# The second expert product in rounded parts, from the 13th tile on

## The chip, the cores and the metric

One core of a Trainium2 chip runs the whole program. The metric is device time in microseconds (us) of that core; lower is better. Engines: PE is TensorE (PEld its weight loads), ACT is ScalarE, DVE is VectorE, POOL is GpSimd, SP issues DMAs.

## What is computed

The input x holds 8 sequences of 512 tokens, 256 wide. First comes x + attention(layernorm(x)), a gated linear attention. The change does not touch it. Then comes a mixture of 8 experts with one expert per token:

```python
aff = x @ centroids.T
assign = jnp.argmax(aff, axis=1)
...
for e in range(nE):
    h = _layernorm(xs, ln_g[e], ln_b[e])
    h = jax.nn.relu(h @ w1[e].T + b1[e])      # 256 -> 1024
    ye = xs + h @ w2[e].T + b2[e]             # 1024 -> 256
    y = y + jnp.where((es == e)[:, None], ye, 0.0)
out_sorted = alpha * y + (1.0 - alpha) * xs
```

Everything is float32. The change is in h @ w2[e].T.

## The kernel before

The attention takes one sequence per step, with up to three sequences in flight. Each finished token is stored as a row of 514 words (normed x, base value, gate, token number) in rows_by_expert, sorted by expert. The second stage, which starts inside the last attention step, takes 39 tiles of 128 rows, all rows of a tile having the same expert. Every engine walks the tiles through its own function turn(t), written out by hand: tiles 0 to 11 one by one among the last attention work, then 20 tiles in a loop of 4 per round, then the last 7 written out. Each instruction waits on semaphores (need), and each engine works strictly in the order in which its turn lists things. In turn(t):

- PE (turn, L1180): up(t+1), 16 products of w1 with the tile's normed rows into bank_a (L1160); z_transposes(t+2), two transposes of gathered rows into bank_b (L1148); down(t), 8 products of 256 columns of h_act with w2_sb into one of two banks bank_l (L1176).
- ACT (turn, L882): relu(t), two ACTIVATEs of 512 columns (L880), then gains(t+2), two of 128 columns that read the transposes (L870).
- DVE (turn, L1565): the first half of bias_h(t+1) (L1548, it reads bank_a into h_sb), finish(t-1) (L1557 adds b2 out of bank_l, L1562 scales and adds the base value), the second half of bias_h(t+1).
- POOL (turn, L673): scatter(n), which waits for finish(n) and stores the tile to out (L667, L670); then gather(n+4), which waits for the same finish and fetches the rows of tile n+4 (L661) into the buffer that finish(n) has read. Four buffers go round.
- SP (fetch_w1, L503): after up(n) is done, 1 MB of w1 for tile n+4 goes into the same of four buffers (L509). w2 of all experts stays in SBUF.

bank_a is single: up(t+1) may write its first half only when bias_h(t) has read it, and so for the second half. h_sb and h_act are single too.

Of the kernel before, what the change touches and what calls it, by code (L numbers as in the profile page):

```python
# [54 lines left out]
def before(s, n):  # L55

    v = s.par - n
    return Step(s.half + v // s.of, v % s.of, s.of)


def number(s):
    return s.half * s.of + s.par


def need(eng, sem, per, s, k):

    base = per * s.par + k + 1
    if not isinstance(s.half, int):  # L70
        eng.wait_ge(sem, s.half * (s.of * per) + base)
    elif s.of * per * s.half + base > 1:
        eng.wait_ge(sem, s.of * per * s.half + base)
# [7 lines left out]
def build_program(nc, x, wq, wk, wv, wo, wg1, wg2, norm_w, centroids_t, ln_g, ln_b, w1_t, b1, w2_t, b2, out):  # L81
# [30 lines left out]
    with ctx:  # L112
        def sb(name, shape, dt):
            return ctx.enter_context(nc.sbuf_tensor(name, shape, dt))

        def sem(name):
            return ctx.enter_context(nc.semaphore(name))
# [2 lines left out]
        w2_sb = sb("w2_sb", [P, E * FC * D], F32)  # L120
        PHASE1_AB = 24576
        ARENA = 33808
        arena_at = nc.sbuf_base
        arena = sb("arena", [P, ARENA], F32)

        class Layout:

# [54 lines left out]
        gathered = [lay3.take(RW + 2)[:, 0:RW] for _ in range(SLOTS)]  # L182
        h_sb = lay3.take(F)
        h_act = lay3.take(F)

        earlier = lay2.take(P)
        is_max = lay2.take(TJ * E)
# [15 lines left out]
        per_tile = lay2.take(7 * TS)  # L205

        k_mix = [sb(f"k_mix{i}", [P, PAIRS * P], F32)[:, :] for i in range(2)]
        b2_sb = lay3.take(E * D)
        ident = sb("ident", [P, P], F32)
        ones = sb("ones", [P, P], F32)  # L210
        masks = sb("masks", [P, LEVELS * NCH * HALF], U8)
# [118 lines left out]
        s_h = sem("h_done")  # L330
        s_hb = sem("h_biased")
        s_hr = sem("h_ready")
        s_ye = sem("y_done")
        s_yb = sem("y_biased")
        s_yo = sem("y_ready")
# [94 lines left out]
        def expert_of(t):  # L430
            if isinstance(t.half, int):
                return tile_expert[0:1, number(t):number(t) + 1]
            return tile_expert[0:1, bass.ds(number(t), 1)]
# [19 lines left out]
        def rounds(eng, turn):  # L453


            with eng.Fori(NA // SLOTS, LAST - 1) as r:
                for i in range(SLOTS):
                    turn(Step(r, i, SLOTS))
            for i in range((LAST - 1) * SLOTS, TILES):
                turn(Step(i // SLOTS, i % SLOTS, SLOTS))  # L460

        def exists(t):

            return not isinstance(t.half, int) or number(t) < TILES
# [233 lines left out]
        def _(act):  # L698
# [163 lines left out]
            def gains(t):  # L862

                if isinstance(t.half, int):
                    act.wait_ge(s_idx, 1 if number(t) < NA else 3)
                e = act.value_load(expert_of(t), min_val=0, max_val=E - 1)
                need(act, s_zt, 1, t, 1)
                need(act, s_h, 2, before(t, 2), 2)
                for i in range(DC):
                    act.activation(xl_t[t.par % 2][:, i * P:(i + 1) * P], bank_b[0][:, i * P:(i + 1) * P], ACT.Identity,  # L870
                                   bias=b_col[:, bass.ds(e * DC + i, 1)], scale=g_col[:, bass.ds(e * DC + i, 1)]).then_inc(s_xl, 1)

            def relu(t):


                need(act, s_ye, 1, t, 0)
                for i in range(2):
                    need(act, s_hb, 2, t, i + 1)
                    w = slice(i * F // 2, (i + 1) * F // 2)
                    act.activation(h_act[:, w], h_sb[:, w], ACT.Relu).then_inc(s_hr, 1)  # L880

            def turn(t):  # L882
                relu(t)
                if exists(before(t, -2)):
                    gains(before(t, -2))

            x_norm(Step(0, 0, 2))
            pipeline(act, step)

            act.wait_ge(s_small, 64)  # L890
            need(act, s_pick, 2 * LEVELS, LAST_SEQ, 2 * LEVELS)
            gains(tile(0))
            gains(tile(1))
# [19 lines left out]
        def _(pe):  # L913
# [251 lines left out]
            def down(t):  # L1165

                p = t.par % 2
                if isinstance(t.half, int):
                    pe.wait_ge(s_idx, 1 if number(t) < NA else 3)
                e = pe.value_load(expert_of(t), min_val=0, max_val=E - 1)  # L1170

                need(pe, s_yb, 1, before(t, 2), 1)
                for k in range(FC):
                    if k % 4 == 0:
                        need(pe, s_hr, 2, t, k // 4 + 1)
                    m = pe.matmul(bank_l[p][:, 0:D], h_act[:, k * P:(k + 1) * P], w2_sb[:, bass.ds(e * (FC * D) + k * D, D)],  # L1176
                                  start=(k == 0), stop=(k == FC - 1))
                m.then_inc(s_ye, 1)

            def turn(t):  # L1180
                if exists(before(t, -1)):
                    up(before(t, -1))
                if exists(before(t, -2)):
                    z_transposes(before(t, -2))
                down(t)

            pe.wait_ge(s_const, 1)
            pe.wait_ge(s_wqk, 32)
# [31 lines left out]
        def _(dve):  # L1220
# [167 lines left out]
            def slots(c):  # L1388

                n = number(c)  # L1390
                need(dve, s_rank, 1, c, 1)
                if n in (EARLY - 1, NSEQ - 1):
                    dve.wait_ge(s_total, 1 + (n == NSEQ - 1))
                    own(dve.tensor_copy(end_e, bank_c[1][:, E * TJ:E * (TJ + 1)]))
                dve.tensor_tensor(by_e(place), bank_c[1][:, 0:E * TJ].rearrange("p (e j) -> p j e", e=E),
                                  hot5[:, :, 1:TJ + 1].rearrange("p e j -> p j e"), ALU.mult).then_inc(s_slot, 1)
                need(dve, s_slot, 2, c, 1)
                dve.tensor_reduce(slot_f[:, n * TJ:(n + 1) * TJ], by_e(place), AX_X, ALU.add).then_inc(s_slot, 1)
# [153 lines left out]
            def finish(t):  # L1552
                p = t.par
                e = dve.value_load(expert_of(t), min_val=0, max_val=E - 1)
                need(dve, s_ye, 1, t, 1)
                need(dve, s_yo, 1, t, 0)
                dve.tensor_tensor(y_sb, bank_l[p % 2][:, 0:D], b2_sb[:, bass.ds(e * D, D)], ALU.add).then_inc(s_yb, 1)  # L1557
                need(dve, s_yb, 1, t, 1)

                if not isinstance(t.half, int) or t.half > 0:  # L1560
                    dve.wait_ge(s_out[p], t.half * 16)
                dve.scalar_tensor_tensor(out=y_out[p], in0=y_sb, scalar=gathered[p][:, 2 * D:2 * D + 1],  # L1562
                                         in1=gathered[p][:, D:2 * D], op0=ALU.mult, op1=ALU.add).then_inc(s_yo, 1)

            def turn(t):  # L1565
                one = before(t, -1) if exists(before(t, -1)) else None
                if one is not None:
                    bias_h(one, 0)
                if not isinstance(t.half, int) or number(t) > 0:
                    finish(before(t, 1))  # L1570
                if one is not None:
                    bias_h(one, 1)

            c = LAST_SEQ
            slots(LAST_BUT_ONE)
            for n in range(2):
                bias_h(tile(0), n)
# [58 lines left out]
```

## Time and profile before

| | us |
|---|---|
| median of 3 runs | 653.22 (652.31 to 654.06) |
| the profiled execution | 650.17 |
| its span | 648.4 |
| PE busy | 593.3 (92%) |
| DVE, ACT, POOL busy | 346.1, 281.5, 260.8 |
| granted TensorE clock, mean share of full speed | 0.975 |

The span runs from the first to the last instruction of the profiled execution; 1.8 us of that execution's time lie around it. The page gives busy time of each engine and groups of instructions by line; the trace can also be asked for a timeline, for windows (busy time, granted clock and DMA share of a stretch) and for single lines. "Idle before <- releaser" on a row tells how long the engine stood still before it and what ended that; "issue" is idle time that no wait explains, such as the reading of a register.

### The profile page before, as it was taken

The page shows a single profiled execution, that of the slowest core. Times are in us where ns is not written, and L with a number is a line of the kernel's source. Part 1 is how long each engine was busy: PE and PEld are TensorE (multiplying, and loading weights), DVE is VectorE, ACT ScalarE, POOL GpSimd, SP SyncE. Part 2 cuts the span into 40 slices and gives each one's busy share as a digit, 9 for nine tenths or more (in the row PEclk, how much of TensorE's full clock was granted, in tenths as well). Part 3 has the DMA queues.
Part 4 walks back from the last instruction along what each step waited for, and adds up shares of the span by engine and source line. Part 5 has one row for each costly group of instructions (what it writes and reads, how often), then busy time and mean ns, then how long its engine had stood idle before and what let it go on. Part 6 is the DMA issues. An engine that isn't in the chain of part 4 may idle for free.

```text
span 648.4 us, 12299 instructions
## 1 busy us (share of the span) xinstructions
PE 593.3 (92%) x3638; PEld 501.8 (77%) x3639; DVE 346.1 (53%) x941; ACT 281.5 (43%) x679; POOL 260.8 (40%) x390
## 2 busy tenths in 40 slices
PE   3888999899999999997789979999999999999991
PEld 2556677686877768776789969988899999998981
DVE  2196895959689695998743354222233322332230
ACT  3454556767665775755352412222222223222220
POOL 7715153553918455463433251332222332233311
PEclk9898999999999999996989999999999999999997
DMA  9910010110403011111696573655554565555200
GB/s 323 407 36 32 2 65 1 66 66 3 131 1 99 1 65 33 67 33 49 173 357 195 179 244 99 222 188 190 192 176 178 186 217 202 176 182 187 112 21 1
DMA packets 25188, 83.60 MB, mean 129 GB/s; under 512 B 3822, under 2 KB 13424, under 8 KB 18993
## 3 DMA queue, kind: packets, MB, share of 16 engines
q1 hardware_dynamic: 16896, 59.57, 26.6%
q0 software_dynamic: 7552, 22.89, 10.4%
q8 instruction: 24, 0.39, 0.3%
q10 hardware_dynamic: 688, 0.52, 0.3%
q14 instruction: 28, 0.22, 0.1%
HBM read 70.35 MB, written 13.53 MB: 129 GB/s over the span
## 4 chain that ended last, share of the span: by engine, by line
PE 76%; DVE 10%; issue 4%; POOL 3%; DMA 3%; ACT 1%; DVEq 0%; ACTq 0%; POOLq 0%
PE bank_l L1176 20%; PE bank_a L1160 19%; PE bank_a L936 7%; PE bank_l L924 6%; PE bank_a L965 5%; DVE arena L1250 4%; PE bank_c L1039 3%; DMA arena<-rows_by_expert,take_idx 2%; PE bank_b L1016 2%; DVE arena L1261 2%; PE bank_a L981 2%; PE bank_a L974 2%; PE bank_b L1015 2%; PE bank_c L1056 2%; PE bank_b L1002 2%
## 5 line engine op out<-in xcount | busy, mean ns | idle before, releaser
L1160 PEld LDWEIGHTS bank_a<-masks,arena 128*128 128x128 f32 x1248 | 146.5, 194 | 1.7
L1548 DVE TENSOR_TENSOR arena<-bank_a,b_col 128x512 f32<-128x512 f32 x78 | 53.9, 691 | 175.6 <-PE bank_a L1160 161.8
L1160 PE MATMUL bank_a<-masks,arena 128*128 128x128 f32 x1248 | 147.2, 277 | 0.0
L1176 PE MATMUL bank_l<-w_sb,arena 128*128 x624 | 143.4, 383 | 4.0 <-issue 3.0
L1176 PEld LDWEIGHTS bank_l<-w_sb,arena 128*128 128x128 f32 x624 | 116.5, 192 | 20.7 <-issue 6.4
L670 POOL DMA_INDIRECT out<-k_mix,put_of x39 | 41.1, 1055 | 178.8 <-DVE k_mix L1562 172.3
L924 PEld LDWEIGHTS bank_l<-arena,k_mix 128*128 128x128 f32 x448 | 65.5, 198 | 45.8 <-ACT k_mix L705 33.4
L880 ACT ACTIVATE arena<-arena 128x512 f32<-128x512 f32 x78 | 44.9, 622 | 106.2 <-PE bank_l L1176 104.6
L1250 DVE TENSOR_TENSOR arena<-arena 128x256 f32<-128x256 f32 x224 | 88.2, 437 | 5.1 <-PE bank_l L924 5.0
L924 PE MATMUL bank_l<-arena,k_mix 128*128 128x128 f32 x448 | 73.5, 290 | 12.4 <-DVE arena L1261 10.6
L936 PE MATMUL bank_a<-arena 128*128 128x512 f32 x160 | 82.0, 612 | 0.0
L870 ACT ACTIVATE masks<-bank_b,b_col,g_col 128x128 f32<-128x128 f32 x78 | 31.5, 453 | 112.4 <-PE bank_b L1148 112.4
L705 ACT ACTIVATE k_mix<-arena 128x128 f32<-128x128 f32 x224 | 61.0, 310 | 38.6 <-DVE arena L1250 38.4
L1261 DVE COPY_PREDICATED arena<-masks,bank_l 128x256 f32<-128x256 uint8 x112 | 51.0, 520 | 0.0
L705 ACT ACTIVATE arena<-bank_a 128x512 f32<-128x512 f32 x40 | 23.8, 594 | 48.0 <-PE bank_a L965 31.4
L609 POOL DMA_INDIRECT rows_by_expert<-arena x32 | 37.5, 1172 | 16.3 <-issue 16.3
L661 POOL DMA_INDIRECT arena<-rows_by_expert,take_idx x39 | 38.9, 998 | 11.9 <-issue 11.9
L936 PEld LDWEIGHTS bank_a<-arena 128*128 128x128 f32 x160 | 26.4, 197 | 9.2 <-issue 8.5
L638 POOL TENSOR_TENSOR arena<-arena 128x512 f32<-128x512 f32 (+6 forms) x56 | 25.6, 458 | 18.5 <-DVE arena L1411 14.6
L965 PE MATMUL bank_a<-arena 128*128 128x256 f32 x128 | 30.7, 396 | 1.9 <-DVE arena L1416 1.9
L1039 PE MATMUL bank_c<-arena 128*128 128x256 f32 x128 | 32.4, 380 | 0.0
L573 POOL TENSOR_SCALAR o_neg_mean<-o_mom 128x4 f32<-128x4 f32 x8 | 2.3, 282 | 73.4 <-issue 61.6
(150 smaller groups left out, 771.0 us busy)
## 6 DMA issues: line engine op xcount, KB each, us to landing
arena<-w SPq DMA_DIRECT2D x39, 1024.0 KB, 4.8
arena<-x SPq DMA_DIRECT2D x16, 512.0 KB, 5.6
w_sb<-w SPq DMA_DIRECT2D x8, 1024.0 KB, 14.3
arena<-b SPq DMA_DIRECT2D x1, 1024.0 KB, 14.1
arena<-rows_by_expert,take_idx POOLq DMA_INDIRECT x39, 3.7
out<-k_mix,put_of POOLq DMA_INDIRECT x39, 4.1
rows_by_expert<-arena POOLq DMA_INDIRECT x32, 4.8
arena<-wk SPq DMA_DIRECT2D x1, 256.0 KB, 3.9
```

Source lines behind the costliest of these rows:

```text
L670: pool.indirect_dma_start(out=out, out_offset=bass.IndirectOffsetOnAxis(ap=put_of[:, n:n + 1], axis=0), in_=y_out[p], in_offset=None, boun ...
L705: return act.activation(dst, src, ACT.Copy)
L880: act.activation(h_act[:, w], h_sb[:, w], ACT.Relu).then_inc(s_hr, 1)
L924: ins = pe.matmul(bank, k_mix[l % 2][:, m * P:(m + 1) * P], level_queries(buf, m, l), start=True, stop=True)
L936: return pe.matmul(bank[:, :], w[:, i * width + h * P:i * width + (h + 1) * P], xn_t[:, i * T:(i + 1) * T], start=(i == 0), stop=(i == DC ...
L965: m = pe.matmul(bank_a[1 - half][:, j * D:(j + 1) * D], xn_t[:, t0:t0 + P], wv_sb[:, i * D:(i + 1) * D], start=(i == 0), stop=(i == DC - 1))
L1039: m = pe.matmul(bank_c[half][:, j * D:(j + 1) * D], o_t[:, t0:t0 + P], wo_sb[:, i * D:(i + 1) * D], start=(i == 0), stop=(i == DC - 1))
L1160: m = pe.matmul(bank_a[k // 4][:, k % 4 * P:(k % 4 + 1) * P], w1_now[t.par][:, i * F + k * P:i * F + (k + 1) * P], xl_t[t.par % 2][:, i * ...
L1176: m = pe.matmul(bank_l[p][:, 0:D], h_act[:, k * P:(k + 1) * P], w2_sb[:, bass.ds(e * (FC * D) + k * D, D)], start=(k == 0), stop=(k == FC ...
L1250: dve.tensor_tensor(half, half, factor(decay[b.par], h, l, second), ALU.mult).then_inc(s_up, 1)
L1261: dve.copy_predicated(picked(attn_t[b.par], l, odd), mask, scores.rearrange("p m (n h) -> p m n h", h=2 ** l)).then_inc(s_pick, 1)
L1548: dve.tensor_tensor(h_sb[:, n * 512:(n + 1) * 512].rearrange("p (k t) -> p k t", t=P), bank_a[n][:, :].rearrange("p (k t) -> p k t", t=P), ...
```

## The change

For tiles 12 to 38 the second product is no longer one float32 product per block but three, with operands of type float32r, the rounded form: h_high by w2_high, h_high by w2_low, h_low by w2_high. ACT's relu writes h_high in place of h_act; ACT's new high_part(t+1) copies the expert's w2 (128x2048) rounded into one of two buffers w2_high, behind gains(t+2). DVE's new w2_low_part(t+1) takes w2 minus w2_high into one of two buffers w2_low, at the head of its turn; then come finish(t-1), both halves of bias_h(t+1), and two h_low_part (relu of h_sb minus h_high, 512 columns each). PE's down_in_parts(t) runs 16 products with h_high and 8 with h_low. Tiles 0 to 11 are computed as before. The new buffers lie in SBUF that the attention has left by then.

```diff
--- before.py
+++ after.py
@@ -120,8 +120,9 @@
...
-        arena_at = nc.sbuf_base
+        arena_at = -(-nc.sbuf_base // 32) * 32
         arena = sb("arena", [P, ARENA], F32)
...
@@ -182,8 +183,16 @@
         gathered = [lay3.take(RW + 2)[:, 0:RW] for _ in range(SLOTS)]
         h_sb = lay3.take(F)
         h_act = lay3.take(F)
+        h_at = lay3.at - F
...
+        lay3.at = dead_at - F
+        h_low = lay3.take_rounded("h_low", F)
+        h_high = nc.alloc_sbuf_tensor_at("h_high", [P, F], F32R, offset=arena_at + 4 * h_at)[:, :]
+        lay4 = Layout(dead_at, PHASE1_AB)
+        w2_high = [lay4.take_rounded(f"w2_high{i}", FC * D) for i in range(2)]
+        w2_low = [lay4.take_rounded(f"w2_low{i}", FC * D) for i in range(2)]
...
+        s_whi = sem("w2_high_ready")
+        s_wlo = sem("w2_low_ready")
+        s_hlo = sem("h_low_ready")
...
@@ -458,6 +471,13 @@
                     turn(Step(r, i, SLOTS))
             for i in range((LAST - 1) * SLOTS, TILES):
                 turn(Step(i // SLOTS, i % SLOTS, SLOTS))
+
+        def in_parts(t):
+
+            return not isinstance(t.half, int) or number(t) >= NA
+
+        def w2_of(e):
+            return w2_sb[:, bass.ds(e * (FC * D), FC * D)]
 
         def exists(t):
 
@@ -877,17 +897,29 @@
                 for i in range(2):
                     need(act, s_hb, 2, t, i + 1)
                     w = slice(i * F // 2, (i + 1) * F // 2)
-                    act.activation(h_act[:, w], h_sb[:, w], ACT.Relu).then_inc(s_hr, 1)
+                    act.activation((h_high if in_parts(t) else h_act)[:, w], h_sb[:, w], ACT.Relu).then_inc(s_hr, 1)
+
+            def high_part(t):
+                e = act.value_load(expert_of(t), min_val=0, max_val=E - 1)
+                if isinstance(t.half, int) and number(t) in (NA, NA + 1):
+
+                    need(act, s_o, 2, LAST_SEQ, 2)
+                    need(act, s_og, 2, LAST_SEQ, 2)
+                need(act, s_ye, 1, before(t, 2), 1)
+                copy(w2_high[t.par % 2], w2_of(e)).then_inc(s_whi, 1)
 
             def turn(t):
                 relu(t)
                 if exists(before(t, -2)):
                     gains(before(t, -2))
+                if exists(before(t, -1)) and in_parts(before(t, -1)):
+                    high_part(before(t, -1))
 
             x_norm(Step(0, 0, 2))
             pipeline(act, step)
 
             act.wait_ge(s_small, 64)
+            act.sem_inc(s_whi, 1 + NA)
             need(act, s_pick, 2 * LEVELS, LAST_SEQ, 2 * LEVELS)
             gains(tile(0))
             gains(tile(1))
@@ -1177,12 +1209,34 @@
                                   start=(k == 0), stop=(k == FC - 1))
                 m.then_inc(s_ye, 1)
 
+            def down_in_parts(t):
+
+                p = t.par % 2
+                need(pe, s_yb, 1, before(t, 2), 1)
+                need(pe, s_whi, 1, t, 1)
+                need(pe, s_wlo, 1, t, 1)
+                for k in range(FC):
+                    if k % 4 == 0:
+                        need(pe, s_hr, 2, t, k // 4 + 1)
+                    h, w = slice(k * P, (k + 1) * P), slice(k * D, (k + 1) * D)
+                    pe.matmul(bank_l[p][:, 0:D], h_high[:, h], w2_high[p][:, w], start=(k == 0), stop=False)
+                    pe.matmul(bank_l[p][:, 0:D], h_high[:, h], w2_low[p][:, w], start=False, stop=False)
+                for k in range(FC):
+                    if k % 4 == 0:
+                        need(pe, s_hlo, 2, t, k // 4 + 1)
+                    m = pe.matmul(bank_l[p][:, 0:D], h_low[:, k * P:(k + 1) * P], w2_high[p][:, k * D:(k + 1) * D],
+                                  start=False, stop=(k == FC - 1))
+                m.then_inc(s_ye, 1)
+
             def turn(t):
                 if exists(before(t, -1)):
                     up(before(t, -1))
                 if exists(before(t, -2)):
                     z_transposes(before(t, -2))
-                down(t)
+                if in_parts(t):
+                    down_in_parts(t)
+                else:
+                    down(t)
 
             pe.wait_ge(s_const, 1)
             pe.wait_ge(s_wqk, 32)
@@ -1562,8 +1616,29 @@
                 dve.scalar_tensor_tensor(out=y_out[p], in0=y_sb, scalar=gathered[p][:, 2 * D:2 * D + 1],
                                          in1=gathered[p][:, D:2 * D], op0=ALU.mult, op1=ALU.add).then_inc(s_yo, 1)
 
+            def w2_low_part(t):
+                e = dve.value_load(expert_of(t), min_val=0, max_val=E - 1)
+                need(dve, s_whi, 1, t, 1)
+                dve.tensor_tensor(w2_low[t.par % 2], w2_of(e), w2_high[t.par % 2], ALU.subtract).then_inc(s_wlo, 1)
+
+            def h_low_part(t, n):
+                need(dve, s_ye, 1, t, 0)
+                need(dve, s_hb, 2, t, n + 1)
+                need(dve, s_hr, 2, t, n + 1)
+                w = slice(n * 512, (n + 1) * 512)
+                dve.scalar_tensor_tensor(out=h_low[:, w], in0=h_sb[:, w], scalar=0.0, in1=h_high[:, w],
+                                         op0=ALU.max, op1=ALU.subtract).then_inc(s_hlo, 1)
+
             def turn(t):
                 one = before(t, -1) if exists(before(t, -1)) else None
+                if one is not None and in_parts(one):
+                    w2_low_part(one)
+                    finish(before(t, 1))
+                    bias_h(one, 0)
+                    bias_h(one, 1)
+                    h_low_part(one, 0)
+                    h_low_part(one, 1)
+                    return
                 if one is not None:
                     bias_h(one, 0)
                 if not isinstance(t.half, int) or number(t) > 0:
@@ -1572,6 +1647,8 @@
                     bias_h(one, 1)
 
             c = LAST_SEQ
+            dve.sem_inc(s_wlo, 1 + NA)
+            dve.sem_inc(s_hlo, 1 + 2 * NA)
             slots(LAST_BUT_ONE)
             for n in range(2):
                 bias_h(tile(0), n)
```

The order of two engines moves. ACT, one tile's turn in the written-out part before (masks is xl_t, bank_b0 holds the transposes, arena is h_sb and h_act):

```order
L880 ACTIVATE arena<-arena 128x512 [waits h_biased,y_done]
L880 ACTIVATE arena<-arena 128x512 [waits h_biased]
L866 TENSOR_LOAD tile_expert [waits indices_ready]
L866 ISA x2
L870 ISA [waits h_done,z_transposed]
L870 ACTIVATE masks<-bank_b0,b_col,g_col 128x128
L870 ISA
L870 ACTIVATE masks<-bank_b0,b_col,g_col 128x128
```

And the same turn of the changed kernel:

```order
L900 ACTIVATE h_high_50<-arena 128x512 [waits h_biased,y_done]
L900 ACTIVATE h_high_50<-arena 128x512 [waits h_biased]
L886 TENSOR_LOAD tile_expert [waits indices_ready]
L886 ISA x2
L890 ISA [waits h_done,z_transposed]
L890 ACTIVATE masks<-bank_b0,b_col,g_col 128x128
L890 ISA
L890 ACTIVATE masks<-bank_b0,b_col,g_col 128x128
L903 TENSOR_LOAD tile_expert
L903 ISA x2
L725 ISA [waits y_done]
L725 ACTIVATE w2_high0_51<-w2_sb 128x2048
```

The copy of w2 for the next tile stands behind the two instructions that wait for the transposes (z_transposed). DVE, one turn before (k_mix is y_out, masks is y_sb):

```order
L1548 TENSOR_TENSOR arena<-bank_a0,b1_col 128x512
L1554 TENSOR_LOAD tile_expert
L1554 ISA x2
L1557 ISA [waits y_ready,y_done]
L1557 TENSOR_TENSOR masks<-bank_l0,arena 128x256
L1562 SCALAR_TENSOR_TENSOR k_mix1<-masks,arena 128x256 [waits rows_out2,y_biased]
L1543 TENSOR_LOAD tile_expert
L1543 ISA x2
L1548 ISA [waits h_done,h_ready]
L1548 TENSOR_TENSOR arena<-bank_a1,b1_col 128x512
```

And in the changed kernel:

```order
L1622 ISA [waits w2_high_ready]
L1622 TENSOR_TENSOR w2_low0_53<-w2_sb,w2_high0_51 128x2048
L1608 TENSOR_LOAD tile_expert
L1608 ISA x2
L1611 ISA [waits y_ready,y_done]
L1611 TENSOR_TENSOR masks<-bank_l0,arena 128x256
L1616 SCALAR_TENSOR_TENSOR k_mix1<-masks,arena 128x256 [waits rows_out2,y_biased]
...
L1602 ISA [waits h_done,h_ready]
L1602 TENSOR_TENSOR arena<-bank_a0,b1_col 128x512
...
L1602 TENSOR_TENSOR arena<-bank_a1,b1_col 128x512
L1629 SCALAR_TENSOR_TENSOR h_low_49<-arena,h_high_50 128x512 [waits h_ready,h_biased,y_done] x2
```

The wait for w2_high_ready now stands ahead of finish and of both halves of bias_h; before, the first half of bias_h was first in the turn.

## Rows read from the trace of the kernel before

**Rows 1.** The page: busy time, share of the span, instructions of each engine.
```profile
PE 593.3 (92%) x3638; PEld 501.8 (77%) x3639; DVE 346.1 (53%) x941; ACT 281.5 (43%) x679; POOL 260.8 (40%) x390
```

**Rows 2.** Windows: length, busy (instructions) by engine, granted clock, DMA share, GB/s.
```profile
429.96:622.86 192.90, 190.34 (x1301) 178.01 (x1300) 59.59 (x104) 50.85 (x104) 60.60 (x77) 1.00 0.51 176
```

**Rows 3.** Timeline, one turn: start, us, engine, line, [idle before <- releaser].
```profile
483.69 3.73 PE L1160 MATMUL bank_a<-masks,arena 128*128 128x128 f32 x32
...
485.79 0.69 DVE L1548 TENSOR_TENSOR arena<-bank_a,b_col 128x512 f32<-128x512 f32 x1 [4.98 <-PE bank_a L1160]
486.64 0.42 DVE L1557 TENSOR_TENSOR masks<-bank_l,arena 128x256 f32<-128x256 f32 x1 [0.16 <-issue]
487.10 0.49 DVE L1562 SCALAR_TENSOR_TENSOR k_mix<-masks,arena 128x256 f32<-128x256 f32 x1
...
487.48 3.62 PE L1176 MATMUL bank_l<-w_sb,arena 128*128 x16
...
487.80 0.81 ACT L870 ACTIVATE masks<-bank_b,b_col,g_col 128x128 f32<-128x128 f32 x2 [2.68 <-PE bank_b L1148]
487.96 0.69 DVE L1548 TENSOR_TENSOR arena<-bank_a,b_col 128x512 f32<-128x512 f32 x1 [0.37 <-issue]
488.46 1.05 POOL L670 DMA_INDIRECT out<-k_mix,put_of  x1 [5.17 <-DVE k_mix L1562]
489.82 1.00 POOL L661 DMA_INDIRECT arena<-rows_by_expert,take_idx  x1 [0.30 <-issue]
```

**Rows 4.** Timeline: gathers that the transposes waited for, and what follows.
```profile
380.68 0.99 POOL L661 DMA_INDIRECT arena<-rows_by_expert,take_idx  x1 [0.30 <-issue]
...
386.74 0.69 PE L1148 MATMUL bank_b<-ident,arena 128*128 128x128 f32 x2 [4.52 <-DMA arena<-rows_by_expert,take_idx]
...
387.59 0.81 ACT L870 ACTIVATE masks<-bank_b,b_col,g_col 128x128 f32<-128x128 f32 x2 [7.75 <-PE bank_b L1148]
...
420.32 1.00 POOL L661 DMA_INDIRECT arena<-rows_by_expert,take_idx  x1 [0.30 <-issue]
...
425.56 0.44 PE L1148 MATMUL bank_b<-ident,arena 128*128 128x128 f32 x2 [0.45 <-DMA arena<-rows_by_expert,take_idx]
...
426.16 0.81 ACT L870 ACTIVATE masks<-bank_b,b_col,g_col 128x128 f32<-128x128 f32 x2 [3.43 <-PE bank_b L1148]
```

**Rows 5.** DMA issues in 470 to 620 us: count, median us to landing.
```profile
arena<-rows_by_expert,take_idx POOLq DMA_INDIRECT x20, 3.6
```

**Rows 6.** Groups by line and shape: busy us, mean ns of one, idle before.
```profile
L705 ACT ACTIVATE k_mix<-arena 128x128 f32<-128x128 f32 x224 | 61.0, 310 | 38.6 <-DVE arena L1250 38.4
L880 ACT ACTIVATE arena<-arena 128x512 f32<-128x512 f32 x78 | 44.9, 622 | 106.2 <-PE bank_l L1176 104.6 <-DVE arena L1548 1.7
...
L1548 DVE TENSOR_TENSOR arena<-bank_a,b_col 128x512 f32<-128x512 f32 x78 | 53.9, 691 | 175.6 <-PE bank_a L1160 161.8 <-issue 13.8
L1557 DVE TENSOR_TENSOR masks<-bank_l,arena 128x256 f32<-128x256 f32 x39 | 16.6, 424 | 14.0 <-issue 7.1 <-PE bank_l L1176 6.0
L1411 DVE SCALAR_TENSOR_TENSOR arena<-arena 128x512 f32<-128x512 f32 x16 | 10.9, 681 | 4.7 <-ACT arena L747 4.7
L1528 DVE CAST masks<-arena 128x3584 uint8<-128x3584 f32 x1 | 2.0, 2016 | 0.0
```

**Rows 7.** Timeline: ACT starting on a result of DVE.
```profile
332.85 0.69 DVE L1548 TENSOR_TENSOR arena<-bank_a,b_col 128x512 f32<-128x512 f32 x1 [2.86 <-PE bank_a L1160]
333.58 0.63 ACT L880 ACTIVATE arena<-arena 128x512 f32<-128x512 f32 x1 [0.50 <-DVE arena L1548]
```

**Rows 8.** Windows of 1 us: PE, PEld, DVE, ACT, POOL busy, granted clock, DMA.
```profile
327.00:328.00 1.00, 0.32 (x2) 0.08 (x2) 0.93 (x6) 0.52 (x2) 0.00 (x0) 1.00 0.98 410
328.00:329.00 1.00, 0.57 (x5) 0.60 (x5) 0.86 (x6) 0.29 (x2) 0.00 (x0) 0.86 1.02 426
329.00:330.00 1.00, 1.00 (x6) 1.00 (x6) 0.39 (x2) 0.80 (x2) 0.79 (x3) 0.50 1.03 434
...
332.00:333.00 1.00, 1.00 (x11) 1.00 (x10) 0.15 (x1) 1.00 (x3) 0.78 (x1) 0.93 1.05 434
```

More of the change, by code:

```diff
@@ L122, in build_program @@
         ARENA = 33808
-        arena_at = nc.sbuf_base
+        arena_at = -(-nc.sbuf_base // 32) * 32
         arena = sb("arena", [P, ARENA], F32)
+        assert nc.sbuf_base == arena_at + 4 * ARENA
         class Layout:
@@ L207, in build_program @@
         k_mix = [sb(f"k_mix{i}", [P, PAIRS * P], F32)[:, :] for i in range(2)]
-        b2_sb = lay3.take(E * D)
+        b2_sb = arena[:, h_at + F:h_at + F + E * D]
+        assert h_at + F + E * D <= dead_at - F
         ident = sb("ident", [P, P], F32)
```

## The prediction

> **What bounds the kernel now.** I read the page's busy times first: PE is busy for 92% of the span, DVE and ACT for about half [rows 1]. That average hides the stage that changes, so the windows come next. From the start of up(12) (429.96) to the start of up(38) (622.86), PE is busy for 190.34 of 192.90 us at full granted clock, and DVE and ACT for 59.59 and 50.85 us [rows 2]. Those are 26 turns of 7.42 us. The timeline of one turn shows what PE does in them: up takes 3.73, the transposes follow, down takes 3.62 [rows 3]. The reader might conclude that only PE's work counts and that the other engines have over 4 us a turn to give. That holds for work that lies beside PE's. So the third view is the order of waits in the turn, and it says otherwise.
>
> **What goes away on PE.** The 16 records of a tile's down take 3.62 us [rows 3], two for each of the 8 float32 products, 0.226 us each. The Trainium skill (FP8 and Floating Point Precision, TensorE Precision Notes) says that true float32 takes four passes through the array and that reduced float32 is cut to a shorter format; no run so far shows the latter. No row has a float32r product. If a record is two passes, one pass is 0.113 us, and 24 of them are 2.7 us; at the other end each costs what a float32 product costs, 0.4525 us, and 24 are 10.9 us. The name "one-pass" lies nearest to the first; it saves 0.9 us a tile, some 24 us over 27 tiles, if PE still sets the pace. Below I find that it doesn't, so the saving is worth nothing.
>
> **What is added.** Copy of w2, 2048 columns on ACT: from 310 ns for 128 columns and 622 for 512 [rows 6] the slope is 0.81 ns a column, hence 622 + 1536 x 0.81 = 1.87 us. Difference of w2 on DVE: from 424 ns for 256 columns and 691 for 512 the slope is 1.04, hence 2.29 us; a single-input cast ran at 2016 / 3584 = 0.56 ns a column [rows 6], which would give 1.15. I take 2.29, since the nearest rows have two inputs like it; 1.15 stays as the lower end. The Trainium skill (VectorE: DVE Perf Modes, Why `tensor_tensor` can't do 2x_2P or 4x) says that the faster mode needs both read ports for one tensor, so that float32 with two tensors keeps one element a cycle; the two-input rows agree at 1.04 ns, and by the cast's rate the total below would be 28 us lower. The two h_low_part are 2 x 0.69 (the 681 ns row) and come right behind the relu, while DVE waits for the next copy: covered. Relu into the rounded form is no longer work than before, by the same engine and width. PE's register load of the expert number goes; it lay under PE's work. SP's fetch of w1 for tile n+4 still waits for up(n) and has three longer turns to land in: no cost.
>
> **Where the added work stands.** The copy for tile t+1 is behind gains(t+2), which waits for the transposes of tile t+2, which PE makes only after up(t+1). The difference for t+1 waits for that copy, and DVE does it before finish(t-1) and before bias_h(t+1). up(t+2) may not write bank_a before bias_h(t+1). So one chain now runs through every turn. From the start of up:
>
> - to the start of gains 4.11 (483.69 to 487.80) and gains 0.81 [rows 3];
> - the expert number is read: DVE shows gaps of 0.16 to 0.37 for such a read [rows 3]; I take 0.35, as gains is short;
> - copy 1.87, handover to DVE 0.05 (0.04 in [rows 7]), difference 2.29;
> - the two instructions of finish 0.95 (486.64 to 487.59), gap 0.37 and bias_h 0.69 [rows 3], PE's start 0.2 (an estimate; PE follows within some tenths where it waited).
>
> The sum is 11.7 us, against 7.42 now. PE's 2.7 us of down lie inside it.
>
> **The second loop, through POOL.** finish(t-1) also releases the buffer into which gather(t+3) fetches. Now the rows come in time with little to spare: where the transposes waited, they began 4.8 to 6.1 us after the gather (420.32 to 425.56, 380.68 to 386.74) [rows 4]; the median landing is 3.6 behind an issue of 1.00 [rows 3, 5], so 4.6. The 6.06 stood beside the stores of rows, which are over by then; I take 4.8, nearest to the median. With finish moved to the end of the chain, the loop from gather to gather is: 4.8 to the transposes; 0.60 to gains (425.56 to 426.16 [rows 4]); gains 0.81, read 0.35, copy 1.87, handover 0.05, difference 2.29, finish 0.95; 0.87 to the store's issue (487.59 to 488.46) and 1.36 from there to the next gather [rows 3]. Sum **13.95 us**. Against up this is the later one: the gather starts about 1.0 us after up does (0.87 + 1.36 less the 1.26 of gap, bias_h and PE's start), so the rows are there at 5.8, when up, done at 3.7, has left PE idle for 2 us. Each step of this loop goes on to the next turn, so nothing catches up.
>
> **The sum.** The first turn has its rows early and takes 11.7; 25 more take 13.95: 360.5. Less 192.9 this is +167.6. Behind the last up the end hardly changes: the last copy waits for no transposes, its chain (1.6 for relu, then 0.35 + 1.87 + 2.29 + 0.95 + two halves of bias_h, relu, h_low, the last 8 products) comes to about 11.7 us, against 11.8 now between up(38) and the end of down(38). Added to the profiled execution's own 650.17, and with 2 us for stretches at the low clock, this gives **820 us**. The runs' median lies 3 us above that execution; I leave it within the range.
>
> **The clock.** PE would be idle for some 2 us before the transposes and 5 us before the next up. The windows show what that can do: after about 2 us with PE mostly idle (busy 0.32 in 327 to 328, 0.57 in the next) the granted clock fell from 1.00 to 0.50, that is from 2.4 to 1.2 GHz, and it was back in 332 to 333 with PE busy [rows 8]. So I expect such falls in most turns. The low stretch there was some 3.4 us long; one like it costs up (3.73) no more than 3.4 / 2 = 1.7 us, and up has 2 us to spare before the rows land: mostly covered, hence the 2 us above.
>
> **Rivals.**
>
> 1. *Rows in time.* If the gather took under about 2.8 us, up would set the turn: 26 x 11.7 = 304, total 762. Against it: no row shows a gather that short [rows 4, 5]. Chance 0.06.
> 2. *The clock stays low.* Then up takes 7.46 and the transposes to gains 0.85 (386.74 to 387.59 [rows 4]): a turn is 11.7 + 3.73 + 0.25 = 15.7, total 650 + 408 - 193 = 865. For it: the fall in [rows 8]; against it: the clock rose again there while PE was busy, and up keeps PE as busy as that. The Trainium skill (TensorE: Matmul & The Clock Gate, HAM oscillation) tells of loops in which PE falls back to half rate in each round's gap; by that rule this rival holds if every up is slow from end to end. Chance 0.12.
> 3. *Not one pass.* If float32r products cost as much as float32 ones, down is 10.9 and PE sets the turn: 3.73 + 0.1 + 10.86 = 14.7 and so 26 x 14.7 = 382, total 839. Nothing in the trace excludes it. Chance 0.08.
> 4. *Faster.* The copy and the difference hide beside PE, and 27 tiles save 0.9 each: about 626. For it: DVE's and ACT's idle time [rows 2]. It decides for this if the path from the transposes to the end of bias_h stays under the 2.9 us of PE work beside it. By the terms above that path is 8.2; with copy and difference at zero it would still be over 4. Chance 0.02.
>
> The forecast itself has 0.70, and 0.02 is for what I don't see.
>
> **Range.** The difference at the lower price takes 26 x 1.14 = 30 off (790); gather at 4.6 takes 5 more (785). Gather at 5.24 adds 11, and falls of the clock that up's slack doesn't cover up to 1 us a turn, 26: with rival 3 at 839 this reaches to 850. Left out are rivals 1, 2 and 4. A measurement of this kernel tells 0.3%, about 2 us, from no change; every case but rival 4 lies far above that: faster 0.02, same 0.01, slower 0.97.
>
> **What would show it.** Right: turns of 14 us between the starts of up; the transposes waiting for DMA about 2 us after up; ACT's 128x2048 copy at 1.9 us starting right behind gains, DVE's at 2.3 us starting on the copy's end, finish and bias_h behind it, and up waiting for DVE for some 5 us; PE busy for under 60% there. Wrong: a difference of 1.2 us; transposes right behind up; PE busy throughout (rival 3 or 4); up at 7 us in every turn (rival 2); or any up that starts before the difference ends.

## The result and the profile after

The changed kernel takes **812.93 us** (median of 4 runs, 811.93 to 815.06), the kernel before 652.76 (4 runs): a ratio of 1.246 with a 95% interval from 1.242 to 1.249. Forecast were 820 and a range from 785 to 850. The profiled execution took 811.93 us, its span is 810.2.

The page of the changed kernel, in the order of [rows 1] and then its granted clock and its costliest new groups (out<-in, count | busy, mean ns | idle before):

```profile
PE 637.1 (79%) x3854; PEld 553.0 (68%) x3854; DVE 442.7 (55%) x1022; ACT 335.8 (41%) x706; POOL 267.0 (33%) x390
...
PEclk9999999999999988999899877777777777777777
...
L1192 PE MATMUL bank_a<-masks,arena 128*128 128x128 f32 x1248 | 204.6, 341 | 120.1 <-DVE arena L1602 120.1
...
L1622 DVE TENSOR_TENSOR w_low<-w_sb,w_high 128x2048 fp32r<-128x2048 f32 x27 | 61.9, 2292 | 184.6 <-ACT w_high L725 184.6
...
L1222 PE MATMUL bank_l<-w_high,h_high 128*128 128x256 f32 x216 | 53.4, 289 | 0.8 <-ACT h_high L900 0.8
L725 ACT ACTIVATE w_high<-w_sb 128x2048 fp32r x27 | 51.7, 1914 | 1.6 <-issue 1.1
```

Up (L1192) now waits 120.1 us in all for bias_h (L1602), and its mean record takes 341 ns where it took 277 in the kernel before (L1160 there, 147.2 us for the same 1248 records). The 216 products of h_high by w2_high are 27 tiles by 8: one record each, where a float32 product had two. The windows, to be held against [rows 2], are from the start of up(13) (441.84) to that of up(38) (783.30), 25 turns:

```profile
441.84:783.30 341.46, 225.22 (x1450) 220.32 (x1451) 146.69 (x175) 99.53 (x126) 65.58 (x76) 0.75 0.29 95
```

A turn is 13.66 us, PE is busy for 66% of it, and the granted clock is 0.75 on the mean. One turn in the timeline, to be held against [rows 3]:

```profile
551.39 5.99 PE L1192 MATMUL bank_a<-masks,arena 128*128 128x128 f32 x32 [4.65 <-DVE arena L1602]
...
552.41 1.28 POOL L681 DMA_INDIRECT arena<-rows_by_expert,take_idx  x1 [0.30 <-issue]
...
557.22 0.38 PE L1180 MATMUL bank_b<-ident,arena 128*128 128x128 f32 x2
...
557.76 0.81 ACT L890 ACTIVATE masks<-bank_b,b_col,g_col 128x128 f32<-128x128 f32 x2 [4.89 <-PE bank_b L1180]
...
558.73 1.92 ACT L725 ACTIVATE w_high<-w_sb 128x2048 fp32r x1 [0.15 <-issue]
...
560.79 2.29 DVE L1622 TENSOR_TENSOR w_low<-w_sb,w_high 128x2048 fp32r<-128x2048 f32 x1 [6.93 <-ACT w_high L725]
...
563.00 0.42 DVE L1611 TENSOR_TENSOR masks<-bank_l,arena 128x256 f32<-128x256 f32 x1
...
564.51 0.69 DVE L1602 TENSOR_TENSOR arena<-bank_a,b_col 128x512 f32<-128x512 f32 x1 [0.46 <-issue]
```

The chain is the forecast one: transposes, gains, copy, difference, then finish, bias_h, and up at 565.25. Two things differ. Up takes 5.99 us, and the transposes have no idle time before them: they follow up, they do not wait for rows. That is so in all 25 turns (no wait before L1180), and up waits for bias_h in every one, 115.6 us in all. The windows of 1 us (columns as in [rows 8]) show why up is slow:

```profile
550.00:551.00 1.00, 0.00 (x0) 0.00 (x0) 0.54 (x2) 0.00 (x0) 0.00 (x0) 0.50 0.00 0
...
554.00:555.00 1.00, 1.00 (x7) 1.00 (x7) 0.00 (x0) 0.00 (x0) 0.04 (x1) 0.50 0.59 103
555.00:556.00 1.00, 1.00 (x7) 1.00 (x7) 0.00 (x0) 0.00 (x0) 0.00 (x0) 0.53 0.41 160
556.00:557.00 1.00, 1.00 (x12) 1.00 (x11) 0.00 (x0) 0.00 (x0) 0.00 (x0) 1.00 0.00 0
...
561.00:562.00 1.00, 0.00 (x0) 0.00 (x0) 1.00 (x1) 0.00 (x0) 0.00 (x0) 1.00 0.53 221
562.00:563.00 1.00, 0.00 (x0) 0.00 (x0) 1.00 (x2) 0.00 (x0) 0.00 (x0) 0.88 0.00 0
563.00:564.00 1.00, 0.00 (x0) 0.00 (x0) 0.86 (x3) 0.00 (x0) 0.00 (x0) 0.50 0.00 0
```

In this turn the clock falls to 1.2 GHz while PE stands idle before up, and comes back to 2.4 when up has run for over 4 us (up from 551.39, full clock from 556).

### The profile page after: what moved, and what is told of

The parts are those of the page before. It is cut to its first block, busy times and chain, and to the rows that moved or that the text cites. A ratio compares the mean times of both kernels' runs of the same rounds, so it can differ in the third digit from the quotient of the medians.

```text
span 810.2 us, 12857 instructions
## 1 busy us (share of the span) xinstructions
PE 637.1 (79%) x3854; PEld 553.0 (68%) x3854; DVE 442.7 (55%) x1022; ACT 335.8 (41%) x706; POOL 267.0 (33%) x390
## 4 chain that ended last, share of the span: by engine, by line
PE 58%; DVE 14%; issue 10%; ACT 8%; DVEq 3%; DMA 2%; ACTq 1%; POOL 1%; POOLq 0%
PE bank_a L1192 23%; ACT w_high L725 6%; PE bank_a L968 6%; PE bank_l L956 5%; PE bank_l L1208 4%; PE bank_a L997 3%; DVE arena L1304 3%; PE bank_c L1071 2%; DVE arena L1602 2%; DVE arena L1315 2%; PE bank_b L1048 2%; PE bank_a L1013 2%; PE bank_a L1006 2%; PE bank_b L1047 2%; PE bank_c L1088 1%
## 5 line engine op out<-in xcount | busy, mean ns | idle before, releaser
L1192 PE MATMUL bank_a<-masks,arena 128*128 128x128 f32 x1248 | 204.6, 341 | 120.1 <-DVE arena L1602 120.1
L1192 PEld LDWEIGHTS bank_a<-masks,arena 128*128 128x128 f32 x1248 | 199.1, 254 | 125.9 <-DVE arena L1602 96.8
L1622 DVE TENSOR_TENSOR w_low<-w_sb,w_high 128x2048 fp32r<-128x2048 f32 x27 | 61.9, 2292 | 184.6 <-ACT w_high L725 184.6
L1602 DVE TENSOR_TENSOR arena<-bank_a,b_col 128x512 f32<-128x512 f32 x78 | 54.0, 692 | 61.0 <-PE bank_a L1192 41.1
L900 ACT ACTIVATE h_high<-arena 128x512 fp32r<-128x512 f32 x54 | 33.9, 630 | 128.5 <-DVE arena L1602 122.5
L1222 PE MATMUL bank_l<-w_high,h_high 128*128 128x256 f32 x216 | 53.4, 289 | 0.8 <-ACT h_high L900 0.8
L725 ACT ACTIVATE w_high<-w_sb 128x2048 fp32r x27 | 51.7, 1914 | 1.6 <-issue 1.1
L1223 PE MATMUL bank_l<-w_low,h_high 128*128 128x256 f32 x216 | 51.1, 278 | 0.0
L1208 PE MATMUL bank_l<-w_sb,arena 128*128 x192 | 46.1, 395 | 0.6 <-issue 0.6
L1208 PEld LDWEIGHTS bank_l<-w_sb,arena 128*128 128x128 f32 x192 | 37.2, 199 | 6.5 <-issue 1.4
L1629 DVE SCALAR_TENSOR_TENSOR h_low<-arena,h_high 128x512 fp32r<-128x512 f32 x54 | 38.4, 715 | 5.7 <-ACT h_high L900 4.8
```

What stands on the lines that cost most here:

```text
L725: return act.activation(dst, src, ACT.Copy)
L1192: m = pe.matmul(bank_a[k // 4][:, k % 4 * P:(k % 4 + 1) * P], w1_now[t.par][:, i * F + k * P:i * F + (k + 1) * P], xl_t[t.par % 2][:, i * ...
L1222: pe.matmul(bank_l[p][:, 0:D], h_high[:, h], w2_high[p][:, w], start=(k == 0), stop=False)
L1223: pe.matmul(bank_l[p][:, 0:D], h_high[:, h], w2_low[p][:, w], start=False, stop=False)
L1602: dve.tensor_tensor(h_sb[:, n * 512:(n + 1) * 512].rearrange("p (k t) -> p k t", t=P), bank_a[n][:, :].rearrange("p (k t) -> p k t", t=P), ...
L1622: dve.tensor_tensor(w2_low[t.par % 2], w2_of(e), w2_high[t.par % 2], ALU.subtract).then_inc(s_wlo, 1)
```

## The experiments

The turn in each is the mean of 25, from the start of up(13) to that of up(38) in the timeline; the ratio is to the kernel before in the same set of runs, with its 95% interval.

| run | median us | ratio | up(13), up(38) | turn |
|---|---|---|---|---|
| the change | 812.93 | 1.246 (1.242 to 1.249) | 441.84, 783.30 | 13.66 |
| warm | 790.82 | 1.216 (1.210 to 1.222) | 441.85, 761.09 | 12.77 |
| low_1536 | 815.97 | 1.254 (1.248 to 1.260) | 445.08, 785.50 | 13.62 |
| low_1024 | 780.82 | 1.193 (1.184 to 1.203) | 447.30, 755.07 | 12.31 |
| warm_finish_first | 721.48 | 1.103 (1.097 to 1.109) | 445.85, 700.67 | 10.19 |
| copy_first | 665.42 | 1.022 (1.017 to 1.027) | 438.60, 638.24 | 7.99 |
| difference_later | 668.90 | 1.024 (1.018 to 1.029) | 441.51, 641.79 | 8.01 |
| both_orders | 629.94 | 0.968 (0.963 to 0.972) | 438.59, 604.85 | 6.65 |
| no_w2_parts | 629.58 | 0.964 (0.959 to 0.969) | 440.92, 606.80 | 6.64 |

### warm: does the clock or the gather set the turn?

```diff
                 if in_parts(t):
                     down_in_parts(t)
+                    if exists(before(t, -1)):
+                        for _ in range(5):
+                            pe.matmul(bank_c[0][:, :], ones[:, :], w2_sb[:, 0:512], start=True, stop=True)
```

> The changed kernel with five extra products (float32, 128x512, ones by w2, into a bank that nobody reads) behind every down of tiles 12 to 37, where PE stands idle. Theory A (the prediction's: the gather loop of 13.95 us sets the turn): PE's clock does not matter, the turn stays at 13.65 and the time at 813. Theory B (up at the low clock sets it): the clock stays at 1.00, up takes 3.8 instead of 6.0, and the turn falls to what is longest at full clock: 12.7 if the rows land 3.6 us after the gather's issue begins (time about 789), 11.8 if they do so earlier than that (767).

Theory B holds: 22 us less, with more work on PE. The timeline of warm:

```profile
558.86 3.84 PE L1192 MATMUL bank_a<-masks,arena 128*128 128x128 f32 x32 [0.42 <-DVE arena L1605]
...
559.89 1.28 POOL L681 DMA_INDIRECT arena<-rows_by_expert,take_idx  x1 [0.30 <-issue]
...
563.60 0.44 PE L1180 MATMUL bank_b<-ident,arena 128*128 128x128 f32 x2 [0.91 <-DMA arena<-rows_by_expert,take_idx]
```

Up takes 3.84, and only now do the transposes wait for the rows, in 24 of the 25 turns. In this turn they begin 3.71 us after the gather's start; in the 12 turns between 455 and 602 us it is 3.57 to 4.27. So the loop through POOL exists, but it is some 12.7 us long, not 13.95, and in the change it lies hidden under a slow up.

### low_1536 and low_1024: a shorter chain

```diff
...
-                dve.tensor_tensor(w2_low[t.par % 2], w2_of(e), w2_high[t.par % 2], ALU.subtract).then_inc(s_wlo, 1)
...
+                dve.tensor_tensor(w2_low[t.par % 2][:, 0:1536], w2_sb[:, bass.ds(e * (FC * D), 1536)],
+                                  w2_high[t.par % 2][:, 0:1536], ALU.subtract).then_inc(s_wlo, 1)
```

Not shown are the lines that fill both buffers in full in the turn of tile 12.

> The changed kernel with VectorE's difference of w2 over 1536 of 2048 columns (the last quarter of w2_low keeps what tile 12's turn put there; the first two buffers are filled in full once, which adds some 4 us once). The chain from the transposes to the next up is 0.53 us shorter per turn. If the turn is a plain sum of its steps, by theory A or B, it falls to 13.1 and the time to 813 - 13 + 4 = 804. Theory C (the turn is tied to the alternation of the clock: a shorter chain brings up earlier into the low stretch, and up gets longer by as much): the turn stays at 13.65 and the time is 813 to 817.

> As low_1536, but the difference covers 1024 of 2048 columns, so that the chain is 1.07 us shorter than in the change. Plain sum: turn 12.6, time 813 - 27 + 4 = 790. Theory C (the turn is tied to the clock's alternation): the tie can only take up what up can give, and up has nearly all of its work in the low stretch in low_1536 already (6.5 of at most 7.5 us); so the tie breaks in at least some turns and the mean turn lies between 12.0 and 13.3, time 776 to 808, with turns of unequal length. A turn of 13.65 again would say that the tie is stronger than that.

low_1536, timeline and one window of 1 us:

```profile
549.77 1.76 DVE L1628 TENSOR_TENSOR w_low<-w_sb,w_high 128x1536 fp32r<-128x1536 f32 x1 [7.36 <-ACT w_high L725]
...
553.59 6.52 PE L1194 MATMUL bank_a<-masks,arena 128*128 128x128 f32 x32 [4.11 <-DVE arena L1604]
```
```profile
552.00:553.00 1.00, 0.00 (x0) 0.00 (x0) 0.54 (x2) 0.00 (x0) 0.00 (x0) 0.71 0.00 0
```

The difference is 0.53 us shorter and up 0.53 longer than the 5.99 above: the turn stays (13.62). The window shows why: the clock falls at about 552.4, 1.2 us before up starts, where in the change it fell at about 562.8, 2.5 us before the up of 565.25. Up has more of the low stretch ahead of it. Theory C holds. With 1.07 us off (low_1024) the tie breaks: single turns lie between 11.4 and 13.3, the mean at 12.31, 1.35 less for 1.07 cut, and up takes from 3.81 to 6.79 us.

### warm_finish_first: is the wait for rows the loop through finish?

As warm, with four extra products, and:

```diff
                 if one is not None and in_parts(one):
-                    w2_low_part(one)
                     finish(before(t, 1))
+                    w2_low_part(one)
```

> The changed kernel with four extra products per turn (clock kept up) and finish(t-1) ahead of the difference in VectorE's turn, so that the gather is released some 7 us earlier and finish is no step of the chain. In warm the transposes wait for the rows; if that wait is the loop from finish to gather, it goes: the turn falls from 12.7 to what the chain from up to bias_h leaves at full clock, 11.8 - 0.95 - 0.4 = 10.5, time about 791 - 25 x 2.2 = 736. If the rows are late for another reason, the turn stays above 12.

It is: the turn is 10.19 and no transposes wait. It is 0.3 shorter than worked out, of which 0.17 shows: in the change 1.43 us lie between the end of the difference and bias_h (563.08 to 564.51), and here the two halves of bias_h start 0.09 before the recorded end of the difference, so 1.52 went and not 1.35.

```profile
566.20 2.29 DVE L1625 TENSOR_TENSOR w_low<-w_sb,w_high 128x2048 fp32r<-128x2048 f32 x1 [4.07 <-ACT w_high L725]
568.40 1.28 DVE L1605 TENSOR_TENSOR arena<-bank_a,b_col 128x512 f32<-128x512 f32 x2
```

The median of 721.48 us is 15 under the expected 736. The shorter turns are worth about 10 of that (25 x 0.4: 2.58 a turn against warm, 2.2 expected); the rest isn't in the turns and stays unexplained. The profiled execution, 729.03 us, was the slowest of the five.

### copy_first and difference_later: one order at a time

copy_first changes ScalarE's turn, difference_later VectorE's:

```diff
                 relu(t)
-                if exists(before(t, -2)):
-                    gains(before(t, -2))
                 if exists(before(t, -1)) and in_parts(before(t, -1)):
                     high_part(before(t, -1))
+                if exists(before(t, -2)):
+                    gains(before(t, -2))
```
```diff
                 if one is not None and in_parts(one):
-                    w2_low_part(one)
-                    finish(before(t, 1))
                     bias_h(one, 0)
+                    finish(before(t, 1))
                     bias_h(one, 1)
+                    w2_low_part(one)
                     h_low_part(one, 0)
                     h_low_part(one, 1)
```

> The changed kernel with ScalarE's copy of w2 ahead of gains, so that it no longer waits for the transposes; VectorE's order is as in the change. The copy then starts behind relu, at about 1.6 us after up starts, the difference ends at 6.0, finish and bias_h end at 8.1: a turn of 8.15 at full clock, time 813 - 3 - 25 x 5.5 = 673. If the order of the copy is not what costs (gather or clock alone set the turn), it stays above 750.

> The changed kernel with VectorE's order alone altered: first half of bias_h, finish, second half, then the difference and the two h_low; ScalarE's copy stays behind gains. up no longer waits for the difference. A loop over two turns is left: transposes, gains, copy, difference, h_low, bias_h, finish, gather, transposes of the tile two on, 0.54 + 0.81 + 0.15 + 1.92 + 0.14 + 2.29 + 1.4 + 1.04 + 1.15 + 2.23 + 3.65 = 15.3, so a turn of 7.7 and about 658. If VectorE's own work sets it, 7.0 and 640. If the copy behind gains alone were enough to do the harm, it is above 750.

Either order alone takes off nearly all of the loss. In copy_first the copy runs beside up. The loop through POOL is still there, as finish stands behind the difference: the transposes wait for rows in all 25 turns, 22.3 us in all, and down stands behind them. Up waits for bias_h for only 1.3 us in all. In the turn shown bias_h ends at 511.51, PE's last product at about the same time, and up starts at 511.57: two chains of nearly equal length, and this run can't tell which of them sets the 7.99.

```profile
503.37 3.84 PE L1192 MATMUL bank_a<-masks,arena 128*128 128x128 f32 x32
...
505.04 1.91 ACT L725 ACTIVATE w_high<-w_sb 128x2048 fp32r x1 [0.19 <-issue]
...
508.32 0.44 PE L1180 MATMUL bank_b<-ident,arena 128*128 128x128 f32 x2 [1.12 <-DMA arena<-rows_by_expert,take_idx]
```

In difference_later nine of the 25 turns take 9.0 to 11.0 us and fourteen 6.6 to 6.9. The long ones are those in which the transposes wait for rows: the loop through finish and gather spans more than one turn. The time is 11 us slower than worked out (668.9 for 658), and the trace shows two things that the working left out. One is POOL, whose work beside the difference is slow in that run (put_of, 0.31 us otherwise; the gather's issue, 1.0); the other is the clock, behind it:

```profile
530.76 2.40 DVE L1624 TENSOR_TENSOR w_low<-w_sb,w_high 128x2048 fp32r<-128x2048 f32 x1 [1.36 <-ACT w_high L725]
531.43 2.41 POOL L687 TENSOR_SCALAR put_of<-arena,skip 128x1 int32<-128x1 f32 x1
...
537.45 2.29 DVE L1624 TENSOR_TENSOR w_low<-w_sb,w_high 128x2048 fp32r<-128x2048 f32 x1 [0.48 <-ACT w_high L725]
538.05 2.56 POOL L681 DMA_INDIRECT arena<-rows_by_expert,take_idx  x1 [0.30 <-issue]
...
543.00 0.69 PE L1180 MATMUL bank_b<-ident,arena 128*128 128x128 f32 x2 [2.34 <-DMA arena<-rows_by_expert,take_idx]
```
```profile
518.00:519.00 1.00, 0.00 (x0) 0.00 (x0) 0.63 (x2) 0.00 (x0) 0.00 (x0) 0.94 0.85 345
519.00:520.00 1.00, 0.67 (x3) 0.67 (x4) 0.69 (x1) 0.00 (x0) 0.36 (x1) 0.50 1.06 442
```

Seven gathers between 450 and 590 us took 2.3 to 3.0 us to issue, and behind each of the seven the transposes waited 2.2 to 2.6 us. The second fence is from such a wait (the transposes start at 519.33): the clock falls to 1.2 GHz in it, and the first of the 24 products behind it start 0.21 us apart instead of 0.12. The waits come to 23.0 us in all; the 25 turns together are 35.8 us longer than 25 of 6.58.

### both_orders: a version faster than either kernel

ScalarE as in copy_first, and in VectorE's turn:

```diff
-                if one is not None and in_parts(one):
-                    w2_low_part(one)
+                if in_parts(t) or (one is not None and in_parts(one)):
                     finish(before(t, 1))
-                    bias_h(one, 0)
-                    bias_h(one, 1)
-                    h_low_part(one, 0)
-                    h_low_part(one, 1)
+                    if in_parts(t):
+                        h_low_part(t, 0)
+                        h_low_part(t, 1)
+                    if one is not None:
+                        bias_h(one, 0)
+                        w2_low_part(one)
+                        bias_h(one, 1)
                     return
```

bias_h also waits for the same half of h_low of the tile before, which reads what it overwrites (in difference_later too).

> Both orders changed. ScalarE: relu, copy of w2 for the next tile, gains. VectorE in the turn of tile t: finish(t-1), h_low of t, first half of bias_h(t+1), difference of w2 for t+1, second half of bias_h(t+1). No step of the added work then stands between the transposes and the next up. If PE sets the turn it is 3.8 + 2.8 = 6.6 us, the time about 632; VectorE's work is 6.3 us a turn and its gaps may make it 7.0, time about 642. If the product in parts cannot pay even so, the time is 653 or more.

> both_orders with the copy and the difference of w2 cut to 128 of 2048 columns from the third tile in parts on (the rest of the buffers keeps what tile 12's turn put there). If both stand fully beside PE's work in both_orders, the turn stays at 6.58 and the time at 630 to 634 (some 4 us come once from filling both buffers). If they still cost, it falls below 625.

both_orders takes 629.94 us, 3.2% less than the kernel before (650.88 in the same set of runs). Its windows over 139 us of the loop, the timeline of one PE turn, and two groups of its POOL and DVE work in 450 to 600:

```profile
459.08:598.43 139.35, 138.71 (x1220) 138.32 (x1220) 118.94 (x147) 78.94 (x105) 92.76 (x63) 1.00 0.56 202
```
```profile
465.50 3.74 PE L1192 MATMUL bank_a<-masks,arena 128*128 128x128 f32 x32
469.07 0.38 PE L1180 MATMUL bank_b<-ident,arena 128*128 128x128 f32 x2
469.21 0.37 PE L1222 MATMUL bank_l<-w_high,h_high 128*128 128x256 f32 x1
469.41 0.28 PE L1223 MATMUL bank_l<-w_low,h_high 128*128 128x256 f32 x1
...
471.12 1.12 PE L1227 MATMUL bank_l<-w_high,h_low 128*128 128x256 f32 x8
472.07 3.74 PE L1192 MATMUL bank_a<-masks,arena 128*128 128x128 f32 x32
```
```profile
L681 POOL DMA_INDIRECT arena<-rows_by_expert,take_idx x23 | 63.9, 2778 | 7.0 <-issue 7.0
...
L1624 DVE TENSOR_TENSOR w_low<-w_sb,w_high 128x2048 fp32r<-128x2048 f32 x23 | 52.7, 2293 | 4.8 <-ACT w_high L725 3.1 <-issue 0.8
```

PE is busy all the time at full clock, DVE for 85% of it. In most turns up starts 6.58 us after the last: 3.57 of up, 0.14 of transposes, 2.86 for 24 products, 0.12 each. no_w2_parts leaves out most of the copy and the difference, so most of its w2 parts belong to another tile's expert and only its time is of use. Its turns from up(14) on are all 6.58, where both_orders has three longer ones (7.12, 6.99, 7.35); together that makes 1.7 us over 24 turns. So the copy and the difference stand beside PE's work but for some 2 us. The mean of 6.64 hides that, since it holds one turn of 7.96 in which the buffers are filled. In no_w2_parts the gather's issue is short again:

```profile
L681 POOL DMA_INDIRECT arena<-rows_by_expert,take_idx x23 | 23.1, 1006 | 7.0 <-issue 7.0
```

## Why the prediction was right, and which steps weren't

- **PE's work isn't what the change moves.** Right. One product in parts is 0.12 us (forecast 0.113), and rival 3 is refuted: 24 of them take 2.86 us, not 10.9. The choice between the two had rested on the name "one-pass", which stands in no row and no view of this case, so that part came true by luck. The saving is real where it is on the path, 6.65 for 7.42 us on the mean in both_orders, but smaller than the 0.9 forecast: most turns fall by 0.66 (7.24 to 6.58), since the 16 float32 records hold PE for 3.45 us from start to next start (487.48 to 490.93), not 3.62. In the change it is worth nothing.
- **The chain through copy, difference, finish and bias_h.** Right, and shown by the runs that cut it: either order alone brings 813 down to 665 or 669. Its terms: copy 1.91 (1.87 forecast), difference 2.29 (2.29), read 0.16 (0.35), gains 0.81, the first turn 11.3 (11.7; up(12) starts at 430.52). For the difference the Trainium skill's rule (VectorE: DVE Perf Modes, Why `tensor_tensor` can't do 2x_2P or 4x) holds, the trace agrees: 2292 ns for 2048 columns, 1.04 ns from one column to the next as in [rows 6], not the cast's 0.56.
- **The second loop, through POOL.** The failed step is "I take 4.8": the transposes can begin 3.71 us after the gather's start, in warm. I had put the issue of 1.00 ahead of the median landing of 3.6 [rows 5]; 3.71 fits a landing that counts from the issue's start. The waits in [rows 4], 5.24 and 6.06 us and not "4.8 to 6.1", were times when the rows came late. The kernel before had rows that spoke against 4.8, transposes that did not wait at all and began 4.32 us after the gather:

```profile
614.87 1.00 POOL L661 DMA_INDIRECT arena<-rows_by_expert,take_idx  x1 [0.30 <-issue]
...
619.19 0.38 PE L1148 MATMUL bank_b<-ident,arena 128*128 128x128 f32 x2
```

With 3.71 the loop is 12.86 by my terms, and 12.77 was measured in warm. Two of the signs listed beforehand failed with this step: the transposes never wait for DMA in the change, and PE is busy for 66%, not under 60.
- **The clock.** "Mostly covered" failed with it: with the rows there 4.7 us after up's start (1.0 + 3.7) in place of 5.8, up's slack is about 1 us, not 2, and each up lost 2.15 (5.99 for 3.84). The low clock costs 22 us (812.93 against 790.82, where the wait for rows is next), and I had 2. This is rival 2 in part: with a mean of 0.75 the clock is low for half of the time, not for all of it. The Trainium skill (TensorE: Matmul & The Clock Gate, HAM oscillation) describes such a round trip in loops with idle gaps; the trace agrees in that it comes back in every turn, and up ran at full clock again within the same turn.
- **The sum.** A turn of 13.66 for 13.95, less 25 x 0.29 = 7 us, is about the whole distance from 820. Two errors cancelled: a loop 1.2 us too long, and a clock whose cost lifted the other loop to almost the same length. The total came out within 1% by luck; the statement of what waits last was wrong. The end behind up(38) grew by 1.4 us (26.9 of span for 25.5), where I had none: up(38) took 6.07 us, and the last relu (792.25) had to wait for the products behind it. Two small slips in the working changed nothing: the lower price of the difference is worth 28 us in one place and 30 in another, and 11 and 26 us on top of 820 give 857, not 850.

## What to carry to other kernels

Idle time of an engine is room only for work that doesn't stand between two waits of the engine that bounds. Before work is given to ScalarE or VectorE, write down behind which wait it is queued, and what is queued behind it; the same copy and difference cost 160 us in one place and some 2 in another. Where a new wait leaves TensorE idle in every round, count the products behind it at the low clock, and try the case with filler products to tell the clock from the wait.

## What the runs showed of the hardware beyond that

**A turn can tie itself to the clock.** In the change the granted clock alternates, and each turn of 13.66 us holds one low and one full stretch (mean 0.75; up at 5.5 to 6.3 us in all 25 turns). When 0.53 us was cut from the chain (low_1536), up began 1.2 instead of 2.5 us behind the fall and took 6.52 instead of 5.99 us; nothing was won. Cutting 1.07 won 1.35. A small saving in such a loop can measure as zero, and that says nothing of the step that was cut.

**POOL's instructions take longer beside VectorE's difference.** The gather's issue takes 2778 ns on the mean in both_orders and 1006 ns in no_w2_parts, where the difference is 128 columns wide. Two turns of both_orders show when:

```profile
455.52 1.01 POOL L681 DMA_INDIRECT arena<-rows_by_expert,take_idx  x1 [0.30 <-issue]
455.58 2.29 DVE L1624 TENSOR_TENSOR w_low<-w_sb,w_high 128x2048 fp32r<-128x2048 f32 x1 [0.50 <-ACT w_high L725]
456.55 1.48 POOL L687 TENSOR_SCALAR put_of<-arena,skip 128x1 int32<-128x1 f32 x1
...
462.46 2.29 DVE L1624 TENSOR_TENSOR w_low<-w_sb,w_high 128x2048 fp32r<-128x2048 f32 x1 [0.16 <-issue]
462.62 3.01 POOL L681 DMA_INDIRECT arena<-rows_by_expert,take_idx  x1 [0.30 <-issue]
```

A gather that started 0.06 us before the difference took its usual 1.01; one that started 0.16 behind its start ended 0.88 behind its end, and so did the others of the 23 in 450 to 600, within 0.02. Whether it is the width, the place of its two operands (both in SBUF) or something else that delays POOL wasn't tried. In both_orders it costs little: PE waits for rows twice, 0.8 us in all.
